# Turned rows and outputs through the score slots to ScalarE; row sums in five groups

## What is computed

```python
    scores = jnp.einsum('bqhd,bkhd->bhqk', q, k) / jnp.sqrt(jnp.asarray(HEAD_DIM, dtype=q.dtype))
    attn = jax.nn.softmax(scores, axis=-1)
    out = jnp.einsum('bhqk,bkhd->bqhd', attn, xv)
...
    attn = jnp.einsum('bhqd,bhkd->bhqk', q, k) * scale
    attn = jax.nn.softmax(attn, axis=-1)
    attn_out = jnp.einsum('bhqk,bhkd->bhqd', attn, v)
```

## Time and profile before

| | |
|---|---|
| median of 3 runs | 7084.32 us (7074.83 to 7091.73) |
| profiled execution | 7082.01 us, of it the span 7080.1 us |
| busy: PE, DVE, ACT, POOL | 87%, 74%, 55%, 25% of the span |
| first attention | about 1694 to 4602 us |
| second attention | about 5000 to 6927 us |
| granted TensorE clock, mean | 0.906 |

### The profile page before, as it was taken

One profiled execution on the slowest core, in us unless ns is written; L12 is line 12 of the kernel. 1 busy time (PEld: TensorE's weight loads), 2 busy tenths in 40 slices (PEclk: granted clock), 3 DMA queues, 4 the chain that ended last, 5 costly groups with the idle time before them and its releaser, 6 DMA issues. The chain is left out here.

```text
span 7080.1 us, 98923 instructions
## 1 busy us (share of the span) xinstructions
PE 6125.6 (87%) x31760; PEld 2758.7 (39%) x31760; DVE 5216.9 (74%) x7383; ACT 3876.2 (55%) x6935; POOL 1753.8 (25%) x954
## 2 busy tenths in 40 slices
PE   5996666776999999999999999955999999999993
PEld 3444442442333333333333333323444444444442
DVE  6996412776888888888888888477777777777755
ACT  4772111112777777777777777611355555555560
POOL 2331100441000000000000000011466666666661
PEclk9998866776999999999999999766899999999996
DMA  4113584544323332333333333076211111111105
GB/s 137 48 48 115 162 300 152 167 166 89 44 45 45 45 48 41 46 47 47 46 46 46 46 46 46 3 222 214 54 37 37 37 37 37 37 37 37 37 6 194
DMA packets 373168, 547.61 MB, mean 77 GB/s; under 512 B 68464, under 2 KB 273200, under 8 KB 352976
## 3 DMA queue, kind: packets, MB, share of 16 engines
q1 hardware_dynamic: 359888, 524.77, 30.7%
q10 hardware_dynamic: 12800, 16.78, 0.7%
HBM read 352.02 MB, written 186.78 MB: 76 GB/s over the span
## 5 line engine op out<-in xcount | busy, mean ns | idle before, releaser
L620 DVE TENSOR_REDUCE at_NM<-at_MX 128x1 f32<-128x1024 f32 (+1 forms) x4096 | 3680.2, 948 | 944.6 <-PE at_MX L494 936.8
L584 ACT ACTIVATE at_PB<-at_S 128x512 f32<-128x512 f32 x6144 | 3227.3, 603 | 1610.0 <-PE at_S L511 1564.6
L494 PE MATMUL at_MX<-at_KT,at_QT 48*128 48x512 f32 (+1 forms) x6144 | 2181.8, 456 | 208.9 <-DVE at_NM L620 129.8
L511 PE MATMUL at_S<-at_QT,at_KT 50*128 50x512 f32 (+1 forms) x6144 | 2330.7, 436 | 29.2 <-ACT at_PB L584 11.9
L511 PEld LDWEIGHTS at_S<-at_QT,at_KT 50*128 50x128 f32 (+1 forms) x6144 | 1086.6, 189 | 1414.0 <-ACT at_PB L584 1276.6
L520 PE MATMUL at_AV<-at_PB,at_VS 128*32 128x512 f32 x12288 | 1635.0, 620 | 0.7 <-ACT at_PB L584 0.7
L460 POOL TENSOR_TENSOR at_SUM<-at_PB 128x2048 f32<-128x2048 f32 x256 | 1198.2, 4680 | 641.9 <-ACT at_PB L584 641.9
L494 PEld LDWEIGHTS at_MX<-at_KT,at_QT 48*128 48x128 f32 (+1 forms) x6144 | 930.3, 190 | 814.3 <-DVE at_NM L620 475.0
L450 POOL CAST at_NMR<-at_NMF 16x128 fp32r<-16x128 f32 x96 | 27.0, 281 | 2921.6 <-DVE at_NMF L629 2921.6
L520 PEld LDWEIGHTS at_AV<-at_PB,at_VS 128*32 128x32 f32 x12288 | 275.1, 110 | 540.2 <-ACT at_PB L584 270.6
L781 PE MATMUL wkv_PQ<-wkv_XT,wkv_WT 128*128 128x512 f32 x768 | 339.5, 599 | 42.8 <-DVE wkv_DL L901 25.8
(11 more groups left out here) (151 smaller groups left out, 3975.0 us busy)
## 6 DMA issues: line engine op xcount, KB each, us to landing
moe_W<-in_w SPq DMA_DIRECT2D x64, 1024.0 KB, 10.4
at_QT<-qk SPq DMA_DIRECT2D x384, 128.0 KB, 5.8
at_KT<-qk SPq DMA_DIRECT2D x384, 128.0 KB, 7.2
qk<-r_HI SPq DMA_DIRECT2D x64, 512.0 KB, 3.6
qk<-r_LO SPq DMA_DIRECT2D x64, 512.0 KB, 4.4
x<-r_X SPq DMA_DIRECT2D x48, 512.0 KB, 3.0
at_VS<-v SPq DMA_DIRECT2D x96, 256.0 KB, 8.6
at_QT<-qk SPq DMA_DIRECT2D x96, 256.0 KB, 4.1
```

What stands on the lines that cost most here:

```text
L494: ins = nc.tensor.matmul(MX[r][:, a, :], QT[u][h:h + NQ, b * P:(b + 1) * P], KT[u][h:h + NQ, (c + a) * W:(c + a + 1) * W], start=True, sto ...
L511: nc.tensor.matmul(SP_[(NSB * s + t) % NSR][:, :], KT[u][h:h + NQ + 2, kb * P:(kb + 1) * P], QT[u][h:h + NQ + 2, c * W:(c + 1) * W], start ...
L584: nc.scalar.activation(PB[:, t % NPB, :], SP_[(NSB * s + t) % NSR][:, :], ACT.Exp, scale=scale).then_inc(exp_done, 1)
L620: nc.vector.tensor_reduce(NM4[:, b, c:c + 1], MX[r][:, :, :].rearrange("p a n -> p (a n)"), AX_X, ALU.max, negate=True).then_inc(ring_got, 1)
```

## The change

Rows of maxima and outputs that were transposed into the ring now go into the score slots S, and ACT copies them out: the maxima to NMF (`take_turned`), the outputs to a new SBUF tile FO (`take_values`). The ring holds maxima alone. Slots are counted by `item`; `occupant` tells whose slot an item takes over, and `slot_free` waits for that one's reader. The turn stands at TURN_AT = 50. In the first attention VectorE's reciprocal and product read FO from SBUF, four steps after the transposes (OUT_STEP + 4).

In the second attention the key blocks form five groups, 0-3, 4-7, 8-9, 10-13 and 14-15. POOL adds block by block to a running total (11 additions a unit), and `sums` stands at 4 x the end of its group + 13: steps 29, 45, 53, and 5 and 13 of the next unit.

```diff
     UNR = 12 if TWO else N
     LOOPS = max(N // UNR - 2, 0)
-    PAIRS = NBLK // 2
+    GROUPS = () if TWO else ((0, 4), (4, 8), (8, 10), (10, 14), (14, 16))
+    NADD = NBLK - len(GROUPS)
...
-    TURN_AT = MX_FROM + 3
-    START = NMX + 1 + EARLY
+    TURN_AT = MX_FROM + 8
...
     def sum_step(i):
 
-        return value_step(2 * i + 1) + 8
+        return NCH * GROUPS[i][1] + LAG + 10
...
+            def add(it, i, kb):
+
+                first = GROUPS[i][0]
+                k = NCH * kb % NPB
+                total = SUM[(len(GROUPS) * it + i) % 2]
+                wait(pool, exp_done, NSB * it + NCH * (kb + 1))
+                if kb == first + 1:
+                    k0 = NCH * first % NPB
+                    wait(pool, l_done, len(GROUPS) * it + i - 1)
+                    other = PB[:, k0:k0 + NCH, :]
+                else:
+                    wait(pool, sum_done, NADD * it + added(kb) - 1)
+                    other = total[:, :, :]
+                nc.gpsimd.tensor_tensor(total[:, :, :], other, PB[:, k:k + NCH, :], ALU.add).then_inc(sum_done, 1)
...
-            def max_turn(it, seq, r):
-                wait(pe, nm_ready, it + 1)
-                wait(pe, ring_got, seq - RING + 1, pe_step)
-                nc.tensor.transpose(MX[r][0:NBLK, 0, 0:P], NM[:, :], ident[:, :]).then_inc(ring_put, 1)
+            def slot_free(n, what, t=0):
+
+                old = occupant(n, what, t)
+                if old is None:
+                    return
+                of, kind, x = old
+                if kind == "score":
+                    wait(pe, exp_done, NSB * of + x + 1, pe_step)
+                elif kind == "turn":
+                    wait(pe, nmf_got, of + 2, pe_step)
+                else:
+                    wait(pe, fo_got, of, pe_step)
+
+            def max_turn(it, r):
+                wait(pe, nm_ready, it + 1, pe_step)
+                nc.tensor.transpose(SP_[r][0:NBLK, 0:P], NM[:, :], ident[:, :]).then_inc(s_put, 1)
...
                 if i == 0:
                     wait(pe, ls_ready, it)
-                wait(pe, sum_done, PAIRS * it + i + 1)
+                wait(pe, sum_done, NADD * it + added(GROUPS[i][1] - 1))
...
+            def take_turned(it, i, r):
+                wait(act, nmr_ready, it)
+                wait(act, s_put, i + 1)
+                nc.scalar.activation(NMF[:, :], SP_[r][0:NBLK, 0:P], ACT.Copy).then_inc(nmf_got, 1)
+
+            def take_values(it, s, i, r):
+                wait(act, norm_done, it - 1)
+                wait(act, s_put, i + 1)
+                nc.scalar.activation(FO[s % 2][:, :], SP_[r][:, :], ACT.Copy).then_inc(fo_got, 1)
...
-                    if TWO and t == OUT_STEP and (not isinstance(n, int) or n > 0):
-                        normalise_turned(n - 1, s + NBUF - 1, *place(n, s, "out"))
-                    if t == TURN_AT and later(n, 1):
-                        take_turned(n + 1, *place(n, s, "turn"))
+                    if TWO and t == OUT_STEP + 4 and (not isinstance(n, int) or n > 0):
+                        normalise_turned(n - 1, s + NBUF - 1)
```

More of the change, by code:

```diff
@@ L298, in places, with item, occupant @@
     def places(n):
-        out = {}
+        out = []
         for t in range(NSB):
-            tile = tile_at(t)
-            if tile and later(n, tile[0]):
-                out["max", tile] = len(out)
+            out.append(("score", t))
             if TWO and t == OUT_STEP and (not isinstance(n, int) or n > 0):
-                out["out", 0] = len(out)
+                out.append(("out", 0))
             if t == TURN_AT and later(n, 1):
-                out["turn", 0] = len(out)
+                out.append(("turn", 0))
         return out
-    def before_window(n):
+    def item(n, s, what, t=0):
+        k = places(n).index((what, t))
         if not isinstance(n, int):
[L314 to L324, removed]
+            return SITEMS * n - TWO + 1 + k, (SITEMS * s - TWO + 1 + k) % NSR
+        i = SITEMS * n - (TWO if n else 0) + 1 + k
+        return i, i % NSR
+    def occupant(n, what, t=0):
+        k = places(n).index((what, t)) - NSR
+        if k >= 0:
+            return (n, *places(n)[k])
+        if isinstance(n, int) and n == 0:
+            return (-1, "turn", 0) if k == -1 else None
+        return (n - 1, *places(n - 1)[k])
+    TAIL = SITEMS * (N - 1) - TWO + 1 + len(places(N - 1))
     with ExitStack() as ctx:
@@ L340, in phase_attention @@
             REC = [m.sb(f"REC{u}", [P, W // P, NCH]) for u in range(2)]
+            FO = [m.sb(f"FO{u}", [P, W]) for u in range(2)]
         else:
@@ L474, in window @@
                     if t == TURN_AT and later(n, 1):
-                        m_parts(n + 1, place(n, s, "turn")[0])
+                        m_parts(n + 1)
             rounds(pool, window)
@@ L552, in outputs @@
                         values(n, s, kb)
-                for i in range(0 if TWO else PAIRS):
+                for i in range(len(GROUPS)):
                     if sum_step(i) == t:
@@ L673, in window @@
                     if tile and later(n, tile[0]):
-                        maxima(n + tile[0], tile[1], *place(n, s, "max", tile))
+                        maxima(n + tile[0], s + tile[0], tile[1])
                     if not TWO:
```

123 lines of the change are left out of this document (63 added, 60 removed).

## The result

The changed kernel takes 6996.03 us, median of 4 runs (6995.52 to 7004.97); the kernel before, beside it on the same chip, 7085.28. The ratio is 0.9878, with an interval of 0.9861 to 0.9896. It is 89 us faster where 221 were forecast: the direction was right, and the time lies 51 us outside the range. The profiled span is 6994.5 us where it was 7080.1.

What follows compares the result with a forecast made beforehand. TensorE's in-order queue was taken to bound the kernel. From 7082.0 us, 72 saved in the first attention and 149 in the second, with 1.5 lost at the end, gave 6862.5, or 6864 against the median; range 6800 to 6945.

Steps and rivals of the forecast that it cites:

- the five groups with sums: Second attention: eight-step groups with row sums apart from the values, bound by TensorE's own time, 6.34 us instead of 7.05.
- The turned maxima: First attention, turn moved to score slots after step 50: 0.15 us over a normal group left, 1.05 a unit gained.
- The outputs' group: First attention, group with transposed outputs: 0.75 us over normal instead of 1.10, a gain of 0.35 a unit.
- The normalisation: First attention: reciprocal and product come four steps later, between two reductions; loss of 0.35 us a unit (0 to 0.67).
- The row's way through POOL and the DMAs: First attention, after the later turn: two POOL instructions and four DMAs fit into the fourteen steps left, about 9 us; hidden.
- the clock in the first attention: First attention: clock drops that followed the old bubbles may get rarer, a gain of 0.1 us a unit.
- The groups without sums: Second attention: three groups of eight steps lose their row sums and last 6.19 us instead of 7.05.
- The hold: Second attention: normalisation with two SBUF inputs waits for POOL's addition, 2.1 us on average; 1.6 a unit with POOL's lag.
- the rival of whole additions: Second attention: the normalisation is held a whole addition each time; units of 57.5 us, 6948 us in all; chance 0.13.
- POOL's pace: Second attention: POOL busy 53.2 us a unit limits the gain; rival with normalisation between additions, units of 53.6, 6828; chance 0.18.
- The rival of "the clock": Second attention: TensorE's clock halved for 17 us of each unit; units of 63.3 us, 7127 us in all; chance 0.08.
- The tail: End of the second attention: the last unit's additions end later, 1.5 us lost.

Runs made afterwards that it cites:

- x5_pairs_apart: The changed kernel, but the second attention has eight pair sums, each three steps behind the values: 7090.31 us, ratio 1.0013.
- x1_nostep: The changed kernel, but the wait of a score for its slot issues no step increment: 6968.56 us, ratio 0.9861.
- x2_rec_psum: The changed kernel, but the second attention's reciprocals go into PSUM tile L, which the product reads; next unit's first sums wait for it: 6947.91 us, ratio 0.983.
- x0_after: The changed kernel once more, unedited, on the chip of the second round of experiments: 7000.0 us, ratio 0.9878.
- x3_pairs_beside: The changed kernel, but the second attention has its eight pair sums again, right beside the values: 7043.36 us, ratio 0.9956.

## Why the prediction was wrong

**The step that failed** is the term of the five groups with sums: "TensorE's own time is then the longer, 1.72 + 0.86 + 8 x 0.47 = 6.34". TensorE's own time is in fact 7.00. In the group from 5708.76 on, values take 1.86 to the next maxima tile, sums 0.99 (5712.22 to 5713.21), and the eight steps 4.15 and not 3.76: the first maxima matmul behind values or sums lasts 0.33 to 0.34 until the next matmul starts and not 0.24, and the last score ahead of either 0.32 to 0.33. It is no wait for the ring: VectorE had been idle for 1.00 us when the tile begun at 5710.62 reached it, and for 0.71 at the one of 5713.21. I had taken the step from the inside of a run of steps, and the 1.72 and 0.86 from values and sums that follow each other without a change of kind. Each excursion from scores to another kind of matmul and back costs some 0.33 us (1.66 from score to score at the sums, 5711.89 to 5713.55, against 0.47 + 0.86), and the change leaves thirteen of them in a unit where eight were. What was gained at the ring was paid here. That gain is real: with sums beside the values, the last steps ahead of the next values take 0.60 us each instead of 0.47, as in the group of the earlier trace rows:

```profile
5736.71 0.50 PE L494 MATMUL at_MX<-at_KT,at_QT 96*128 96x512 f32 x1
...
5737.31 0.50 PE L494 MATMUL at_MX<-at_KT,at_QT 96*128 96x512 f32 x1
```

and in the split group they take 0.47. Three such steps make 0.39, one more excursion 0.33. 5 x 0.66 x 31 is 102 us of the 134 that the span lacks. x5_pairs_apart shows it: 7.0 apart, 7.05 beside. What TensorE does in such a change isn't shown, only what it costs.

**The second miss** is the loop. I read the groups of the first attention from steps, and went over `slot_free` without asking what `pe_step` makes of a wait in a loop. It was priced at nothing and costs 0.06 us a group, 0.9 us in a typical looped unit, 25 us in all; x1_nostep shows it.

**What was right.** The turned maxima: 0.20 left over normal, 0.15 forecast (2.88 as the median over units). The outputs' group: 0.82 over normal, 0.75 forecast (medians 3.49 and 2.67). The normalisation loses 0.14 (2.81) in written-out units, under the 0.35, and 0.35 in the loop of x1_nostep (2.96 against 2.61). The gains fall short although what is left is about right, because the prediction read its rows from the loop and took 2.61 as normal everywhere: in written-out units the turn had cost 1.05 and the outputs 1.00 over their 2.67. Written-out units: 0.91 saved where 1.15 was forecast; 27 of them make 25 us, and 36 looped ones 0.32 x 36 = 12, which are the 36.7. The row's way through POOL and the DMAs is hidden, as forecast.

**Right in kind, too small** was the clock in the first attention, put at 0.1. In the kernel before, ten of the looped units are 1.2 to 4.7 us longer than 44.0: six with the excess at the turned maxima and in the group behind, four where the loop begins anew. The longest group with the turn takes 5.61 us. Its windows, kernel before, first the bubble and then what follows:

```profile
2364.00:2368.00 4.00, 2.73 (x13) 0.58 (x12) 2.94 (x4) 1.79 (x4) 0.73 (x2) 0.73 0.01 2
2368.00:2372.00 4.00, 4.00 (x20) 1.65 (x16) 2.34 (x2) 2.08 (x4) 0.00 (x0) 0.50 0.05 12
```

Without that bubble the changed kernel has no such unit but where the loop begins anew. That is why its mean falls by 0.32 in the loop although its median rises by 0.2.

The groups without sums: 6.16 to 6.22, forecast 6.19. **The hold**: it comes 31 times in 32, with a median of 3.9 us, nearer to the rival of whole additions (4.7) than to the mean of 2.1 that was taken. The prediction's "half of an addition on average" took for chance what the order of the steps fixes. Its net cost was forecast as 1.6, and x2_rec_psum measures 1.6. That is luck: it comes out of a hold of 3.2 us, not of 2.1, and of drops of the clock that appear when the hold is gone. With the 2.9 for reciprocals, copies and the rest that makes 4.5. Measured over normal groups: 0.48 + 1.46 + 2.44 = 4.4 in groups 1 to 3. So the sum of these terms was right, and 50.3 + 3.3 + 4.4 = 58.0 is the unit (57.8 by medians, 57.9 by the mean).

The rule of the Trainium skill ("SBUF — State Buffer", section "SBUF: two separate sides") holds here, where it says held and where it doesn't. The product with two SBUF inputs stands until the addition is over (3.9 us), that with a PSUM input doesn't (0.68, x2_rec_psum), nor does the reciprocal with a single SBUF input (0.94 by the median of the 93 that lie wholly under additions, and 0.94 of the 66 in the kernel before that meet none). The first attention's product, 0.43 us, isn't held, as was said. That the product would in turn hold POOL for as long as it runs is not shown: 17 additions start in the last 0.3 to 0.4 us of a product and take 4.73 us where 4.62 is usual.

**POOL's pace** of 53.2 us was never reached, since TensorE stayed slower:

```profile
L472 POOL TENSOR_TENSOR at_SUM<-at_SUM,at_PB 128x2048 f32<-128x2048 f32 x192 | 888.7, 4628 | 65.7 <-ACT at_PB L611 48.9
L472 POOL TENSOR_TENSOR at_SUM<-at_PB 128x2048 f32<-128x2048 f32 x160 | 749.5, 4685 | 143.9 <-ACT at_PB L611 142.8
```

The additions take what the earlier trace rows said, those onto a running total a little less, and they wait for ACT; the row sums wait for POOL 9.7 us in the whole kernel. The rival of "the clock" didn't come: 0.98 instead of 0.99 in the second attention. The tail lost 6.2 us instead of 1.5. The 10 us of the last unit of the first attention are a gain that wasn't forecast and that the change doesn't explain: that unit takes 55.9 us here (with a granted clock of 0.63 in the window above) and 60.1 in x0_after, which is the same kernel, 55.9 in x1_nostep, 66.2 in the kernel before, 66.5 and 66.6 in x2_rec_psum and x3_pairs_beside, and 58.8 to 61.7 in the others.

Together, in the span: 219.5 forecast (72 + 149 - 1.5) and 85.6 measured. The second attention gave 50.5 instead of 149, 98.5 less, which the 102 of the groups with sums fill. The first gave 36.7 instead of 72, 35.3 less: 25 for the loop's waits, 0.24 x 27 = 6.5 for what the written-out units fell short, and the rest for the looped ones, which even without those waits (x1_nostep, 1.02 saved by the mean) stay 0.13 short. The tail lost 4.7 more, the stretches around the attentions 5.4, and the last unit gave back 10.4: 98.5 + 35.3 + 4.7 + 5.4 - 10.4 = 133.5.

**Open** is why the last unit of the first attention takes anything from 56 to 67 us, also in two runs of one kernel (55.9 and 60.1), and why stages that were not touched differ by up to 13 us between runs (ahead of the first attention 1706.3 to 1719.4), almost all of the 0.2% that I had put down. A few us in the whole time can't be told from that; the lengths of units can.

## What to carry to other kernels

Price a step that is moved by what stands on both sides of it in the queue: work of another kind in the middle of a steady run of matmuls costs its own time and a change in and out, and a stall that it was to fill may be smaller than that. When a wait is rewritten, look at the loops as well as at the straight code: in the trace a wait that is an instruction of its own has a row, and its count per unit shows what became of it. Where VectorE has to work beside long GpSimd instructions, one operand in PSUM takes it out of their way.

## What was unexpected in the hardware

- TensorE loses some 0.33 us at an excursion from 128-column scores to values or sums, four matmuls side by side in the array's columns, and back; 7.00 us without a wait where the sum of the parts was 6.34.
- In the loop, a wait with an increment is a 51 ns row in TensorE's queue, and makes the matmul behind it start 0.14 us after its releaser's end instead of 0.05.
- After 1.35 us of standing still within 3 us, the granted clock was 0.57 for 4 us, and 16 matmuls took 3.62 us instead of 1.93. The same stall was followed by a drop at once in nine units of 16. The drop costs nothing where the hold covers it, some 1.4 us where it comes behind the hold, and 1.2 to 1.9 us in x2_rec_psum (8.21 to 8.93 against 7.05): who takes away a stall sees the next one only then.
